# Six forward scans per super block instead of 32, reordered by ScalarE, and one gathered column in four taken by TensorE in every group

## What is computed

```python
f_out = leaky_relu(f_ni[src] + f_nj[dst] + f_fij + bias, 0.2)   # nf@W_ni, nf@W_nj, ef@W_fij
e = einsum('ehd,hd->eh', f_out, attn)
a = softmax of e over the edges of each dst                     # segment max, exp, segment sum
h = segment_sum((nf @ W_node)[src] * a, dst)
nf, ef = h.mean(heads), f_out.mean(heads)                       # input of the next layer
```

## Time and profile before

| | |
|---|---|
| runs | 2992.46 us median of 3 (2990.29 to 3013.71) |
| profiled execution | span 3006.7 us, from the first to the last instruction |
| VectorE | busy 2490.5 us (83%) |
| TensorE | busy 2404.8 us (80%), mean granted clock 0.843 of full speed |
| GpSimd | busy 2058.9 us (68%), of which 1889.3 us in 1995 gathers |
| ScalarE | busy 1447.6 us (48%) |
| chain that ended last | PE 39%, DVE 29%, issue 14%, ACT 9% |

### The profile page before, as it was taken

The page is one execution under the profiler, slowest core; times in us unless marked ns, Lnnn a source line. Parts: engine busy times, 40 slices in busy tenths (PEclk is TensorE's granted clock), DMA queues, the critical chain, the costliest instruction groups (busy, mean ns, idle before and its releaser), DMA issues.

```text
span 3006.7 us, 50077 instructions
## 1 busy us (share of the span) xinstructions
PE 2404.8 (80%) x15871; PEld 1878.0 (62%) x16027; DVE 2490.5 (83%) x6428; ACT 1447.6 (48%) x3416; POOL 2058.9 (68%) x2167
## 2 busy tenths in 40 slices
PE   3388888888887378888888887649999888998984
PEld 1366667676764356667766665337777777776753
DVE  7399999999997468998999998637888888879784
ACT  0155555555555135555556555414445454445452
POOL 6777777777770577777777776377776666667653
PEclk9699988888899589987999999857778787778796
DMA  6235454535342324343435342332333343333222
GB/s 252 64 96 156 122 147 116 152 110 158 110 128 85 112 74 142 119 149 110 157 111 158 110 153 98 118 103 67 100 120 99 98 136 98 108 108 100 91 92 81
DMA packets 139275, 353.92 MB, mean 118 GB/s; under 512 B 43895, under 2 KB 96027, under 8 KB 120207
## 3 DMA queue, kind: packets, MB, share of 16 engines
q1 hardware_dynamic: 67216, 296.09, 27.9%
q0 software_dynamic: 68960, 39.71, 8.6%
q10 hardware_dynamic: 2838, 14.91, 1.3%
HBM read 137.79 MB, written 212.77 MB: 117 GB/s over the span
## 4 chain that ended last, share of the span: by engine, by line
PE 39%; DVE 29%; issue 14%; ACT 9%; POOL 5%; DMA 3%; SPq 1%; DVEq 0%; ACTq 0%; POOLq 0%
DVE U L1349 12%; PE f_ps L695 12%; PE pick_ps L664 10%; PE f_ps L704 9%; PE xT_ps L685 5%; DVE rows L1266 4%; DVE lr L1277 4%; DVE U L1334 3%; POOL rows L554 2%; ACT f_low L850 2%; ACT xT L841 2%; ACT up L901 2%; PE f_ps L714 2%; ACT wide_ps L889 1%; DVE rows L1378 1%
## 5 line engine op out<-in xcount | busy, mean ns | idle before, releaser
L554 POOL DMA_INDIRECT rows<-nf_tab,src_sb x1995 | 1889.3, 947 | 706.9 <-issue 574.9
L704 PEld LDWEIGHTS f_ps<-w_out,lr 128*128 128x128 f32 x4836 | 701.0, 210 | 379.0 <-issue 277.3
L664 PE MATMUL pick_ps<-nf_part,z 125*128 125x160 bf16 x6345 | 630.0, 264 | 258.4 <-issue 217.0
L1349 DVE TENSOR_TENSOR_SCAN U<-wide_ps,U 128x272 f32<-128x272 f32 (+2 forms) x1272 | 801.6, 694 | 3.2 <-ACT wide_ps L889 2.4
L695 PE MATMUL f_ps<-xT,w_edge 97*128 97x512 f32 x1212 | 753.8, 708 | 22.6 <-ACT ef_new L872 12.0
L664 PEld LDWEIGHTS pick_ps<-nf_part,z 125*128 125x128 bf16 x6345 | 564.6, 112 | 289.8 <-issue 241.3
L704 PE MATMUL f_ps<-w_out,lr 128*128 128x36 f32 (+1 forms) x4836 | 649.8, 274 | 31.2 <-DVE lr L1277 28.8
L1277 DVE TENSOR_TENSOR lr<-f_ps,f_low 128x512 f32<-128x512 f32 x606 | 410.0, 677 | 252.4 <-ACT f_low L850 247.0
L850 ACT ACTIVATE f_low<-f_ps 128x512 f32<-128x512 f32 x606 | 361.0, 596 | 495.9 <-PE f_ps L695 495.9
L685 PE MATMUL xT_ps<-ident,rows 128*97 128x128 f32 x2418 | 431.8, 305 | 76.8 <-issue 37.2
L841 ACT ACTIVATE xT<-xT_ps 97x512 f32<-97x512 f32 x606 | 358.8, 592 | 147.8 <-PE xT_ps L685 145.6
(11 more groups left out here) (163 smaller groups left out, 1070.5 us busy)
## 6 DMA issues: line engine op xcount, KB each, us to landing
u_tab<-up SPq DMA_DIRECT2D x144, 1088.0 KB
s_nd<-edge_first SPq DMA_DIRECT2D x48, 768.0 KB
rows<-nf_tab,src_sb POOLq DMA_INDIRECT x1995, 2.5
ef_tab<-ef_new SPq DMA_DIRECT2D x32, 768.0 KB
ef_st<-ef_tab SPq DMA_DIRECT2D x32, 768.0 KB
z<-fifth_tab SPq DMA_DIRECT2D x141, 96.0 KB
edge_first<-s_nd ACTq DMA_DIRECT2D x16, 768.0 KB
ef_st<-in_edge_attr_dram SPq DMA_DIRECT2D x16, 672.0 KB
```

The lines of the kernel that those rows point to most:

```text
L554: eng.indirect_dma_start(rows[q % RING][:, c * K:c * K + D], None, nf_tab[:, :], bass.IndirectOffsetOnAxis(ap=src_sb[:, t:t + 1], axis=0)) ...
L664: mm = eng.matmul(pick_ps[:, i * PB:(i + 1) * PB], hot[m % 2][0:NQ, f * PW + i * P:f * PW + (i + 1) * P], nf_part[a][0:NQ, f * PB:(f + 1) ...
L704: mm = eng.matmul(f_ps[n % 2][:, u * m:(u + 1) * m], lr[y][:, u * P:(u + 1) * P], w_out[l][:, 0:m], start=True, stop=True)
L1349: last = eng.tensor_tensor_scan(uh[:, c0 * w:c1 * w], dbc[h % 2][:, 0:(c1 - c0) * w], uh[:, c0 * w:c1 * w], 0.0, ALU.mult, ALU.add)
```

## The change

Two parts.

**Target features.** For each super block ScalarE copies `first3` in two halves of 16 features, features outermost, into a work tile (`lay_first`; the value carried in from the left goes into an extra first column, `led`). VectorE runs six scans over 6, 5, 5, 6, 5 and 5 features at once (`fill_dst`, slots 0, 1, 2, 5, 6 and 7), in place; the multiplier `same_w` is 0 in the extra column, so that a scan starts anew at each feature. ScalarE copies the halves into `rows` (`put_dst`, slots 3 and 8). `slice_b` is split: `widen_same` fills the multiplier for six features (slot 0), `slice_cut` fills the cut values at the first `soften` of a super block (slot 4).

**Picks.** Batches of three columns now come from three groups in a row instead of three of four: 62 batches a layer instead of 47, 186 columns instead of 141, and GpSimd gathers 620 columns a layer instead of 665. The filling matmuls of the steady loop go, as long as there are picks. The first pick of a batch moves behind `scores(g)`, and `make_hot` and `pick_rows` go by g % 3 instead of g % 4. One more batch is made ahead.

```diff
+FILL_DS = (6, 5, 5)
+LAY_AT = 3
+PUT_AT = 8
+FILL_AT = {0: (0,), 1: (1,), 2: (2,), 5: (3,), 6: (4,), 7: (5,)}
@@ TensorE
-                    for b in range(2):
+                    for b in range(PICK_LEAD):
@@
                         turn(g + 2)
-                        b, i = g // GB + 2, g % GB
-                        if g >= 0 and i < PICK and b < NPICK:
+                        b, i = g // PICK + PICK_LEAD, g % PICK
+                        picking = g >= 0 and b < NPICK
+                        if picking and i:
                             pick(b, i)
-                        elif g >= 1:
+                        elif not picking and g >= 1:
                             warm(g + 1, FILL_STEADY)
                         if g + 1 >= 0:
                             edges(g + 1)
                         if g >= 0:
                             scores(g)
+                        if picking and not i:
+                            pick(b, i)
@@ ScalarE
-                        if g >= 0 and g % GS == 2 and g // GS + 1 < NS:
-                            put_ef(g // GS + 1)
+                        s, a = g // GS + 1, g % GS
+                        if g >= 0 and a == 2 and s < NS:
+                            put_ef(s)
+                        if g >= 0 and a == LAY_AT and s < NS:
+                            put_dst(s, 0)
+                            lay_first(s, 1)
+                        if g >= 0 and a == PUT_AT and s < NS:
+                            put_dst(s, 1)
+                        if g >= 0 and a == GS - 1 and s + 1 < NS:
+                            lay_first(s + 1, 0)
@@ VectorE
-                        for d in ds:
-                            before = (nf_d1[:, d:d + 1] if s == 0 else
-                                      rows3[(q - 1) % RING][:, SUP - 1, DST0 + d:DST0 + d + 1])
-                            eng.tensor_tensor_scan(rows3[q % RING][:, 0:w, DST0 + d],
-                                                   same_b[q % 2][:, 0:w],
-                                                   first3[q % 2][:, 0:w, d], before,
-                                                   ALU.mult, ALU.add).then_inc(dst_spread, 1)
+                        part = fill_of(s, h)[:, c:c + n]
+                        eng.tensor_tensor_scan(part, same_w[:, 0:n], part, 0.0,
+                                               ALU.mult, ALU.add).then_inc(filled, 1)
@@
+                        if sub_at(b) % SUP == 0:
+                            slice_cut(sub_at(b) // SUP)
@@
-                        if g >= 0 and i == PICK - 1 and b + 3 < NPICK:
-                            pick_rows(b + 3)
-                        if g >= 0 and i == 0 and b + 4 < NPICK:
-                            make_hot(b + 4)
+                        m, at = g // PICK + PICK_LEAD, g % PICK
+                        if g >= 0 and at == PICK - 1 and m < NPICK:
+                            pick_rows(m)
+                        if g >= 0 and at == 0 and m + 1 < NPICK:
+                            make_hot(m + 1)
```

More of the change, by code:

```diff
@@ L30 @@
 PICK = 3
+PICK_LEAD = 3
 PARTS5 = 5
@@ L169, in egat_kernel @@
         nf_d1 = sb("nf_d1", [P, D])
+        DH = sum(FILL_DS)
+        FW = DH * (SUP + 1)
+        runs = sb("runs", [P, FW])
         m_spread = sb("m_spread", [P, H * P])
@@ L204, in egat_kernel @@
         runs_ps = ps("runs_ps", [P, GT * P])
-        same_b = [runs_ps[:, s * SUP:(s + 1) * SUP] for s in range(2)]
         CUTW = SUBS * H * W1
-        cut_b = [runs_ps[:, 2 * SUP + s * CUTW:2 * SUP + (s + 1) * CUTW] for s in range(2)]
+        cut_b = runs_ps[:, 0:CUTW]
+        SAME_D = max(FILL_DS)
+        same_w = runs_ps[:, CUTW:CUTW + SAME_D * (SUP + 1)]
         dcol = up[0][:, 0:T + 1].bitcast(I32)
@@ L274, in egat_kernel @@
         sliced = sem("sliced")
+        cut_made = sem("cut_made")
+        laid = sem("laid")
+        led = sem("led")
+        filled = sem("filled")
         dst_spread = sem("dst_spread")
@@ L339, in picks @@
         def picks(g):
-            return g % GB < PICK and g // GB < NPICK
+            return g < PICK * NPICK
         def is_picked(t):
@@ L357, in by_head, with fill_of @@
             return a[:, 0:H * (w + 1)].rearrange("p (h t) -> p h t", t=w + 1)
+        def fill_of(s, h):
+            return U[h][:, 0:FW] if s == 0 else runs[:, :]
         def cut_at(b):
@@ L361, in cut_at, with fifths_to @@
             return sum(H * (sub_w(a) + 1) for a in range(b) if sub_at(a) // SUP == s)
+        def fifths_to(b):
+            return 8 if b < 0 else min(10 + GB * b // PICK, NPICK)
         def ef_stores_to(q):
@@ L484, in _ @@
                         eng.wait_ge(prep, 7)
-                    for b in range(IDXB + 2):
-                        load_fifths(l, b)
+                    for m in range(6):
+                        load_fifths(l, m)
                     load_first(q0)
                     load_first(q0 + 1)
+                    for m in range(6, 8):
+                        load_fifths(l, m)
                     for s in range(NS):
@@ L496, in _ @@
                             store_u(k0 + b)
-                            if b + IDXB + 2 < NPICK:
-                                load_fifths(l, b + IDXB + 2)
+                            for m in range(fifths_to(b - 1), fifths_to(b)):
+                                load_fifths(l, m)
                     for b in range(SUBS * (NS - 1) + 1, NB):
@@ L833, in put_ef, with lay_first, put_dst @@
                                        ACT.Copy).then_inc(ef_put, 1)
+                    def lay_first(s, h):
+                        q, w = l * NS + s, sup_w(s)
+                        to3 = fill_of(s, h)[:, 0:DH * (w + 1)].rearrange("p (d t) -> p d t", d=DH)
+                        c = DST0 + h * DH
+                        eng.wait_ge(first_in[q % 2], 16 * (q // 2 + 1))
+                        if s:
+                            eng.wait_ge(dst_spread, 2 * q + h)
+                            before = rows3[(q - 1) % RING][:, SUP - 1, c:c + DH]
+                        else:
+                            eng.wait_ge(d1_in, l * 16 + 16)
+                            before = nf_d1[:, h * DH:(h + 1) * DH]
+                        eng.activation(to3[:, :, 0:1], before.rearrange("p (d o) -> p d o", o=1),
+                                       ACT.Copy).then_inc(led, 1)
+                        eng.activation(to3[:, :, 1:w + 1],
+                                       first3[q % 2][:, 0:w, h * DH:(h + 1) * DH]
+                                       .rearrange("p t d -> p d t"), ACT.Copy).then_inc(laid, 1)
+                    def put_dst(s, h):
+                        q, w = l * NS + s, sup_w(s)
+                        c = DST0 + h * DH
+                        eng.wait_ge(filled, FILLS * q + FILLS // 2 * (h + 1))
+                        if q >= RING:
+                            eng.wait_ge(turned, groups_to(q - RING))
+                        eng.activation(rows3[q % RING][:, 0:w, c:c + DH],
+                                       fill_of(s, h)[:, 0:DH * (w + 1)]
+                                       .rearrange("p (d t) -> p t d", d=DH)[:, 1:w + 1, :],
+                                       ACT.Copy).then_inc(dst_spread, 1)
                     def take_xT(g):
@@ L908, in lay_out @@
                                        ACT.Copy).then_inc(up_ready, 1)
+                    lay_first(0, 0)
+                    lay_first(0, 1)
                     put_ef(0)
+                    put_dst(0, 0)
+                    put_dst(0, 1)
+                    lay_first(1, 0)
                     kl = l * NB - 1
@@ L937, in _ @@
                     put_ef(NS - 1)
+                    put_dst(NS - 1, 0)
+                    lay_first(NS - 1, 1)
                     for g in (END, END + 4):
@@ L950, in _ @@
                             lay_out(k - 1)
+                            put_dst(NS - 1, 1)
                         take_xT(g + 2)
@@ L1387, in _ @@
                     pick_rows(1)
-                    slice_b(0)
-                    spread_dst(0, range(D))
+                    make_hot(3)
+                    pick_rows(2)
+                    widen_same(0)
+                    for i in range(FILLS):
+                        fill_dst(0, i)
                     for g in range(-1, END - 2):
@@ L1410, in _ @@
                             if a == 0:
-                                slice_b(s)
-                            ds = range(a * DSTEP, min((a + 1) * DSTEP, D))
-                            if len(ds):
-                                spread_dst(s, ds)
+                                widen_same(s)
+                            for i in FILL_AT.get(a, ()):
+                                fill_dst(s, i)
                     leaky(END - 1)
@@ L1423, in _ @@
                         product(b)
+                        if g == END:
+                            for i in range(3, FILLS):
+                                fill_dst(NS - 1, i)
                         leaky(g + 1)
```

79 lines of the change are left out of this document (41 added, 38 removed).

## The result

The changed kernel takes 3290.98 us (median, 3286.81 to 3293.83), the kernel before 3001.52 us in the same comparison: a ratio of 1.0928 with a 95% interval of 1.0877 to 1.0979. The profiled execution has a span of 3291.9 us, 285 us more than the 3006.7 us of before.

The account below looks back on a forecast made before the run. VectorE's list was taken to set the pace. New idle time of 5.0 us less 0.6 us of work a super block gave +200 us, GpSimd -15, clock +45; with 14 us taken off, 3220 us, range 3070 to 3340.

Parts of the forecast that it names:

- the chains behind `soften` and `add_up`: ScalarE's work up to the next `leaky` or `lower`: 2.10 us behind `soften`, 1.54 us behind `add_up`, uncovered at some slots.
- 0.7 us at slot 0: VectorE idle at slot 0: TensorE's chain from `pick_rows` to `leaky` takes 4.5 us against 3.8 us of VectorE work.
- 1.5 us for the clock: Layers 0 and 1: longer waits at the first pick lower TensorE's clock, 1.5 us a super block.
- VectorE's work: Per super block: scans removed -7.5, new scans +4.0, `widen_same` +0.3, fourth batch of picks +2.6; sum -0.6 us.
- ScalarE's copies: Four copies of 768 elements at 0.82 us each and two of 16: some 3.5 us added a super block.
- Idle time behind the slots: VectorE waiting at `leaky`: chain length less remaining cover at slots 4, 8, 10 and 0; 5.0 us new a super block.
- The clock: TensorE's clock falls behind longer waits for the first pick: 45 us in layers 0 and 1.
- The rival that let the clock in layers 0 and 1 fall as low as in layer 2: TensorE's clock in layers 0 and 1 costs 160 us instead of 45: 3335 us; chance 0.23.
- Layer 2 keeps its price: Layer 2 goes on paying 6.4 us a super block for TensorE's lower clock, with nothing added for the clock.
- GpSimd and the starts: Fewer gathers give 10 us at the starts of layers 1 and 2, a shorter fill some 2 us a layer: -15 us.
- The faster rival: VectorE's work sets the pace and its idle time stays where it was: 2910 us; chance 0.10.
- The rival of the same time: New idle time at `leaky` is partly absorbed, 5.0 us becoming about 1: 2980 to 3010 us; chance 0.07.

Follow-up runs that it names:

- e6_straight: The changed kernel with ScalarE's reordering copies reading and writing without a reorder, so target features come out in the wrong order; 3256.5 us, ratio 1.0811.
- e7_rows_first: The changed kernel with `pick_rows` moved on VectorE from the end of an iteration to just behind its `leaky`; 3288.95 us, ratio 1.0923.
- e13_soften_only: The changed kernel with `pick_rows` just behind `leaky` and only `weigh` and `widen` of heads 0 and 1 moved behind the next `lower`; 2996.88 us.
- both orders: `lower` ahead of `weigh` and `widen` on ScalarE, `pick_rows` just behind `leaky` on VectorE; the kernel before with these two edits took 2888.96 us, ratio 0.9602.
- e5_filled_wait: The changed kernel with six matmuls that nobody reads on TensorE ahead of the first pick of a batch; 3232.02 us, ratio 1.0744.
- e8_both_orders: The changed kernel with `lower` ahead of `weigh` and `widen` on ScalarE and `pick_rows` just behind `leaky` on VectorE; 2892.02 us, ratio 0.9591.

## Why the prediction came out as it did

The side, the range and the chains behind `soften` and `add_up` were right; the forecast of 3220 us lay 71 us below the 3291 measured. The term that was furthest off is TensorE's: late behind the first pick it costs 4.3 us of idle time a super block in layer 1, where the sum had 0.7 us at slot 0 and 1.5 us for the clock. That layer 2 grew by less than forecast cancels a part of this, and that was luck. Of the 71 us, 55 lie in the span (3291.9 for 3237); most of the rest is the 14 us taken off because the profiled run of before lay above the median, while this one lies 1 us above it.

- **VectorE's work.** Forecast -0.6 us, measured +0.1 (47.06 to 47.13 us a super block). The parts are near: the fill alone -2.7 for -3.2, the picks alone +2.5 for +2.6. The new scans were right (0.765 and 0.652 us, 4.1 for 4.0 in all); `widen_same` took 0.45 us where the old copy took 0.20, 0.25 more for the 0.3 forecast. What was mis-sized are the scans removed: 7.46 us is their own busy time, but from start to start four of them take 0.85 us (1522.18 to 1523.03), 6.8 us for 32.
- **ScalarE's copies: mis-sized by a factor of two.** I interpolated 0.82 us by element count; they took 1.58 and 1.54. The step that failed was to take rows with short strides as neighbours of copies that reorder; the copy without a reorder takes 0.84 us, so the interpolation was right for that. The Trainium skill ("ScalarE: Activation LUTs", Rules for kernel authors) budgets about 0.3 us for an instruction with its bias as a pointer operand and 0.83 ns an element, an estimate of 0.94 us for 768. The straight copies took 0.1 us less than that, the reordering ones 0.6 us more. The price to the time was 35 us by `e6_straight`, and not at the slot where I put it.
- **Idle time behind the slots** (forecast, then the mean of layer 1): slot 4 2.10 and 2.02; slot 8 1.55 and 1.99; slot 10 1.54 and 1.48; slot 0 0.7 and 2.15; slot 2 none and none; slot 6 none and 1.37; slot 3 none and 0.75. The three chains on ScalarE were right; 0.44 at slot 8 is the slow `put_dst`. At slots 0, 3 and 6 TensorE is late at the lower clock: from the end of `pick_rows` to `leaky` it takes 6.0, 5.7 and 7.0 us. I had set 4.5 us, the chain at full clock, against VectorE's work, found it covered at slots 3 and 6, and put the lower clock beside it as one lump of 1.5 us.
- **The loop.** The waits do lie on one chain: followed back from a `leaky` by what released each step, it goes through ScalarE behind slots 4, 8 and 10, through `pick_rows`, first pick, `turn`, second pick, `edges` and `lower` behind slots 0, 3 and 6, and through VectorE's list in between. So 58.0 us are 47.1 of work, 9.9 of idle time at `leaky` and 1.0 of smaller gaps. What can't be done is to take one wait out and leave the others as they are: `e6_straight` gave its gain back to slower picks, `e7_rows_first` to lost cover. Where TensorE no longer waits for the bank, the terms add up (`e13_soften_only`).
- **The clock.** Forecast 45 us; filling the waits gave 59 us back on balance. The rival that let the clock in layers 0 and 1 fall as low as in layer 2 did not come true: the granted clock is 0.85 there, not the 0.79 of layer 2 before. But its 3335 us are nearer to the time measured than my 3220, since the waits for TensorE were longer than I had them.
- **Layer 2 keeps its price: wrong.** The 55.2 us there became 58.0, like the other layers (+2.8, not +4.4); with both orders the kernel before takes 48.7 us in layer 2 too, at a granted clock of 0.93 instead of 0.79. What I called the price of the clock was waiting that the orders remove. This cancels a part of the miss of 1.4 and 1.8 us a super block in layers 0 and 1.
- **GpSimd and the starts, -15 us.** The first 36 groups took 49 us longer in the three layers, where three super blocks at the steady difference of each layer (7.3, 7.6 and 2.8 us) make 53. So the starts gave about 4 us, not 15. The last 22 groups, which the sum left out, took 18 us longer. GpSimd waits for `turn` 553.9 us, as forecast: its relief was worth nothing.
- **The faster rival** said that VectorE's work alone would count. The Trainium skill ("Perfetto Trace Analysis", Optimizing Scalar/DVE Operations) says that larger operations, and handing work to ScalarE, can help where VectorE is saturated. The fill alone does both, and took 2.7 us a super block off VectorE; in layers 0 and 1 that gave nothing, and 0.8% in all. In the change the picks bring the work back. With both orders the rival's condition, idle time under 0.9 us, is met, at 2892 us; that this is near its 2910 us is chance, since the kernel before takes 2889 us with the same orders. The rival of the same time was wrong too: nothing was absorbed, the idle time grew by 7.3 us, not 5.0.

## What to carry to other kernels

Before work is taken off or put on a saturated engine, look at what the old instructions covered: here `make_hot`, `pick_rows` and short scans stood between a chain's start and its end on another engine, and moving them uncovered 2 us at a time. Where an engine's list waits early for something that is late and holds back something that is due (here `weigh` ahead of the next `lower`), reorder that list first; with the move of `pick_rows` it was worth 4% on the kernel before, and more on the changed one. And where an edit moves work as well as taking out a wait, it may uncover as much as it wins (`e7_rows_first`): compare the idle time place by place, and try both orders together, before either is judged by the time alone.

## What the runs showed of the hardware

- On ScalarE a copy of 768 elements a partition that exchanges two inner dimensions takes 1.54 to 1.58 us in the changed kernel, about 2.0 ns an element, as long as `put_ef`'s copy of 1536 elements in runs of 32 (1.52 us). Without the exchange it takes 0.84 to 0.86 us (`e6_straight`).
- A scan over 294 elements that starts anew by a zero multiplier takes 0.765 us, near the 0.732 us of `add_up`'s scan of 289 in the same kernel. Two of these and four of 245 (0.652 us) replace 32 scans of 48 elements at 0.21 us each from start to start.
- In layer 1 of the changed kernel the first pick of a batch took 2.16 us behind waits of 1.4 to 2.5 us (36 of 47, lower clock, 1.2 GHz) and 1.20 us behind waits of 0.95 us (11 of 47, 2.4 GHz). With the waits filled, 30 of 47 took 1.20 us (`e5_filled_wait`).
- With TensorE's wait for the bank gone, the mean granted clock did not rise but fell, 0.819 to 0.797 (`e7_rows_first`); its waits at `edges` for `ef_new` grew from 41.5 to 66.8 us in the twelve super blocks of layer 1. Why the clock fell is open. With both orders it is 0.877 (`e8_both_orders`).
